# A three-stage transformer kernel: another order and algebra in the feed-forward chain, three PSUM banks for rolled keys, and a router layer placed in the second attention's drain

## The chip, the cores and the metric

The kernel runs on one core of one Trainium2 chip. The metric is device time in microseconds (us) of one execution. A core has five engines that each work through their own queue in order and wait for each other by semaphores: PE (TensorE, matmul), DVE (VectorE), ACT (ScalarE), POOL (GpSimd) and SP, which here only issues DMAs. Matmul results land in PSUM, eight banks of 128 partitions by 512 floats.

## What is computed

The input is 16 sequences of 256 tokens, each a row of 128 floats. Four residual steps follow each other, each on a layer-normalised x.

```python
x = x + attn_a(_layernorm(x))     # 16 heads of 64, causal
x = x + ffn(_layernorm(x))
x = x + attn_b(_layernorm(x))     # in each token its 16 heads of 8 attend to each other
x = x + ffn(_layernorm(x))        # the same weights
```

The feed-forward step routes tokens to 64 slots per sequence, updates the slots with a gated cell, lets the slots attend to each other, and reads them back:

```python
h = gelu(concat([x, slot_mean]) @ w1 + b1)
route_logits = (h @ w2 + b2) / (abs(tau) + 0.1)
topk_vals, topk_idx = top_k(route_logits, 8)
alpha = (one_hot(topk_idx, 64) * softmax(topk_vals)[..., None]).sum(-2)
si = einsum('bts,btd->bsd', alpha, x) / (alpha.sum(1) + 1e-8)[..., None]
i_r, i_z, i_n = split(si @ Wih.T + bih);  h_r, h_z, h_n = split(S @ Whh.T + bhh)
r, z = sigmoid(i_r + h_r), sigmoid(i_z + h_z);  n = tanh(i_n + r * h_n)
S_new = (1 - z) * n + z * S
attn = softmax((S_new @ wq + bq) @ (S_new @ wk + bk).T * DQ**-0.5)
y = S_new + attn @ (S_new @ wv + bv)
slot_values = (layernorm(y) * ln_g + ln_b) @ wvp + bvp
out = (alpha @ slot_values) @ wo + bo
```

## The kernel before

The program is four stages in a row: the first attention (a_tensor and its sisters for the other engines, 16 batches of 4 head groups), the feed-forward stage f_tensor/f_scalar/f_vector/f_gpsimd (called with rep 0), the second attention (b_tensor and sisters, 16 batches, written two to a loop trip), and the feed-forward stage again (rep 1). x stays in SBUF as the tile X, 32 token tiles of 128 by 128.

**What sets the order.** Each engine walks the same hand-written list of steps (a_steps, b_steps, A_PROLOGUE, A_EPILOGUE, B_PROLOGUE, B_EPILOGUE, F_PLAN) and emits its own part of a step, so the lists are the order of every queue. Nothing moves a step at run time: an instruction whose semaphore is late holds back all that is queued behind it on its engine.

**The feed-forward stage** works in two chunks of 8 sequences (16 token tiles). The steps per chunk are: "stats" and "apply" (layer norm of x into f_xs), "hidden" (transposes, first router layer, gelu), "logits", "top" (eight largest, subtract the largest, mark them), "alpha" (exponential and normalisation), "read" (alpha times x, and alpha transposed), "slots", "inputs" (si transposed, times Wih), "gates", "candidate", "new" (the new slots f_sn), "qkv", "scores", "probs", "attend", "ynorm", "values" and "out". F_PLAN lets the chunks alternate, with chunk 1 two steps behind from "gates" on.

Between the first attention and the feed-forward stage stand set_tensor and set_vector: ten small matmuls and some twenty DVE instructions that derive constants from the weights. The statistics of the first 16 tiles ("ffn_stats", "ffn_apply", in the function early_norm) are taken inside the attention stages, the others in the feed-forward stage.

**The second attention** multiplies the query with keys rolled by whole heads. A "roll" step is four PE matmuls into T[j % 2], one of two banks, and one DVE multiplication out of it (b_prod). Two "dots" steps per batch sum the products, each into a bank of its own, M[j]; ACT copies them out, "flip" transposes them. Values are weighed on POOL ("weigh") and summed on DVE ("gather"). The result b_o goes through a scratch tensor in DRAM and comes back in another layout (b_y); "yt" turns it on PE, "project" and "finish" project it, "add" writes X.

**The drain of the second attention** (B_EPILOGUE) ends with two such turnings. The second waits for POOL's last product, its normalisation and the round trip through DRAM.

## Time and profile before

| | us |
|---|---|
| median of 3 runs | 945.12 |
| lowest, highest | 944.6, 946.56 |
| the profiled execution | 945.51 |
| its span, first to last instruction | 943.7 |
| first attention, to the first router transpose | 524.2 |
| feed-forward stage, to the last add | 90.9 |
| second attention, to the router's first transpose | 233.9 |
| feed-forward stage again, with the output | 94.7 |

The profiled execution lies 0.4 us above the median, and 1.8 us of it are outside the span. The profile shows per engine when an instruction ran, how long the engine had been idle before it, and which engine's semaphore ended that idle time. All times below are us from the start of the span. The matmul clock that was granted is given as a share of 2.4 GHz: 1.00 is 2.4 GHz, 0.50 is 1.2 GHz.

### The profile page before, as it was taken

What the parts mean: (1) busy time and instruction counts of PE and PEld (TensorE: products, weight loads), DVE (VectorE), ACT (ScalarE), POOL (GpSimd) and SP (SyncE); (2) the same over time, 40 slices, a digit from 0 to 9 for tenths busy, and PEclk for the clock granted to TensorE, in tenths of its full rate; (3) what the DMA queues carried; (4) which work ended last, traced back from release to release, by engine and by line L of the source; (5) the groups of instructions that cost most, each with busy time, mean ns of one, the idle gap of its engine ahead of it and who ended that gap; (6) DMA issues with size and microseconds to landing.
All of it is one profiled execution on the core that took longest, in us unless ns stands there. A gap on an engine that the chain in (4) does not pass through costs nothing.

```text
span 943.7 us, 25617 instructions
## 1 busy us (share of the span) xinstructions
PE 789.8 (84%) x10324; PEld 606.5 (64%) x10324; DVE 672.3 (71%) x1528; ACT 480.2 (51%) x849; POOL 409.8 (43%) x302
## 2 busy tenths in 40 slices
PE   1899999999999999999986876667888888839655
PEld 0688888888888888888875553534555555525435
DVE  3767667776677766677674776536999999966773
ACT  1678766787767777677752423013444433315220
POOL 1454444544445444454442100116888888751000
PEclk9999999999999999999996778768999999958786
DMA  6000000000000000000000000000221111120002
GB/s 274 1 3 1 0 0 0 0 0 0 0 0 0 0 0 0 0 0 0 1 1 2 0 1 1 1 0 1 23 24 22 22 22 22 20 27 1 1 1 89
DMA packets 71588, 13.25 MB, mean 14 GB/s; under 512 B 66432, under 2 KB 70528, under 8 KB 70912
## 3 DMA queue, kind: packets, MB, share of 16 engines
q1 hardware_dynamic: 71552, 12.76, 6.2%
q8 instruction: 24, 0.39, 0.2%
q14 instruction: 12, 0.10, 0.0%
HBM read 8.56 MB, written 4.19 MB: 14 GB/s over the span
## 4 chain that ended last, share of the span: by engine, by line
PE 63%; DVE 19%; ACT 8%; issue 5%; POOL 3%; DMA 1%; DVEq 0%; ACTq 0%; SPq 0%; POOLq 0%
PE PS L533 6%; PE PS L490 6%; PE PS L349 5%; PE PS L350 4%; PE PS L351 4%; PE PS L426 3%; PE PS L732 3%; DVE b_prod L843 3%; PE PS L722 3%; PE PS L526 2%; PE PS L512 2%; PE PS L724 2%; PE PS L1015 2%; DVE a_nm L607 2%; PE PS L497 2%
## 5 line engine op out<-in xcount | busy, mean ns | idle before, releaser
L640 POOL TENSOR_TENSOR a_pl<-a_p,a_ph 128x1024 f16<-128x1024 f32 (+1 forms) x128 | 210.7, 1646 | 256.3 <-ACT a_ph L562 256.3
L891 POOL TENSOR_TENSOR b_w<-b_v,b_e 128x2048 f32<-128x2048 f32 x32 | 137.8, 4307 | 13.9 <-ACT b_e L811 13.9
L559 ACT ACTIVATE a_p<-PS 128x1024 f32<-128x1024 f32 (+1 forms) x128 | 103.7, 810 | 74.8 <-PE PS L497 74.7
L607 DVE TENSOR_REDUCE a_nm<-PS 128x4 bf16<-128x512 f32 (+1 forms) x128 | 121.5, 949 | 0.0
L843 DVE TENSOR_TENSOR b_prod<-PS,b_qt 128x512 f32<-128x512 f32 x128 | 85.4, 682 | 26.3 <-PE PS L724 22.0
L562 ACT ACTIVATE a_ph<-PS 128x1024 f16<-128x1024 f32 (+1 forms) x128 | 103.1, 805 | 0.0
L552 ACT ACTIVATE a_qk_h<-PS 128x512 f16<-128x512 f32 x128 | 73.4, 604 | 57.1 <-PE PS L351 55.8
L372 POOL TENSOR_TENSOR veps<-mv,eps 128x2 f32<-128x2 f32 (+2 forms) x40 | 8.0, 201 | 190.4 <-DVE mv L1165 136.9
L596 DVE TENSOR_TENSOR a_qk_l<-PS,a_qk_h 128x512 f16<-128x512 f32 x128 | 87.0, 681 | 3.4 <-ACT a_qk_h L552 3.4
L512 PE MATMUL PS<-a_vh,a_ph 128*128 128x65 f16 x768 | 78.5, 196 | 0.3 <-issue 0.3
L514 PE MATMUL PS<-a_vl,a_ph 128*128 128x64 f16 x768 | 78.3, 194 | 0.0
L516 PE MATMUL PS<-a_vh,a_pl 128*128 128x65 f16 x768 | 78.0, 195 | 0.0
L349 PE MATMUL PS<-xhl,a_wqk_h 128*128 128x256 f16 x256 | 70.8, 277 | 8.5 <-ACT xhl L550 7.5
L512 PEld LDWEIGHTS PS<-a_vh,a_ph 128*128 128x128 f16 x768 | 70.5, 98 | 11.1 <-issue 9.5
L858 DVE TENSOR_REDUCE b_s<-b_w 128x128 f32<-128x2048 f32 x32 | 72.8, 2277 | 4.9 <-POOL b_w L891 4.9
L722 PE MATMUL PS<-b_kh,w_rolls 128*128 128x256 f16 x256 | 65.9, 285 | 11.4 <-DVE b_prod L843 8.0
L603 DVE TENSOR_TENSOR a_vl<-PS,a_vh 128x512 f16<-128x512 f32 x64 | 44.3, 692 | 41.8 <-ACT a_vh L555 41.8
L514 PEld LDWEIGHTS PS<-a_vl,a_ph 128*128 128x128 f16 x768 | 71.4, 100 | 0.1
L516 PEld LDWEIGHTS PS<-a_vh,a_pl 128*128 128x128 f16 x768 | 71.4, 98 | 0.0
L351 PE MATMUL PS<-xhl,a_wqk_l 128*128 128x256 f16 x256 | 70.4, 275 | 0.0
L350 PE MATMUL PS<-xhl,a_wqk_h 128*128 128x256 f16 x256 | 70.3, 275 | 0.0
L724 PE MATMUL PS<-b_kl,w_rolls 128*128 128x256 f16 x256 | 65.3, 283 | 0.0
(225 smaller groups left out, 2038.7 us busy)
## 6 DMA issues: line engine op xcount, KB each, us to landing
scratch_dram<-b_o SPq DMA_DIRECT2D x32, 64.0 KB, 3.6
b_y<-scratch_dram SPq DMA_DIRECT2D x16, 128.0 KB, 2.1
out_dram<-X SPq DMA_DIRECT2D x2, 1024.0 KB, 3.9
w_rest<-rest_dram SPq DMA_DIRECT2D x1, 1862.0 KB, 15.2
X<-x_dram SPq DMA_DIRECT2D x1, 1792.0 KB, 11.2
w_first<-first_dram SPq DMA_DIRECT2D x1, 1600.0 KB, 7.1
w_rolls<-rolls_dram SPq DMA_DIRECT2D x1, 544.0 KB, 15.8
X<-x_dram SPq DMA_DIRECT2D x1, 256.0 KB, 3.6
```

Of the source, the lines that this page charges most:

```text
L349: pe.matmul(dst, ah, bh, start=start, stop=False, skip_group_check=True)
L350: pe.matmul(dst, ah, bl, start=False, stop=False, skip_group_check=True)
L351: return pe.matmul(dst, al, bh, start=False, stop=stop, skip_group_check=True)
L512: pe.matmul(O[q][:, h * W:(h + 1) * W], ph[:, nx, par, pair, at], a_vh[:, (g - 1) % GA, k, h, :], start=first, stop=False, skip_group_chec ...
L514: pe.matmul(O[q][:, h * W:h * W + EA], ph[:, nx, par, pair, at], a_vl[:, (g - 1) % GA, k, h, :], start=False, stop=False, skip_group_check ...
L516: ins = pe.matmul(O[q][:, h * W:(h + 1) * W], pl[:, nx, par, pair, at], a_vh[:, (g - 1) % GA, k, h, :], start=False, stop=h == 3 and k == ...
L559: act.activation((a_p0, a_p1)[j][:, me, :, :, :].rearrange("p a h q -> p a (h q)"), TT[:, :, 0:512 - 256 * j], ACT.Exp, scale=EA ** -0.5)
L562: act.activation((a_ph0, a_ph1)[j][:, me, :, :, :].rearrange("p a h q -> p a (h q)"), TT[:, :, 0:512 - 256 * j], ACT.Exp, scale=EA ** -0.5 ...
L607: dve.tensor_reduce(a_nm[:, nx, j, :].rearrange("p (a h) -> p a h", a=2)[:, :, 0:2], MM[:, :, 0:256 * (j + 1)].rearrange("p a (h k) -> p a ...
L640: pool.tensor_tensor(*(n[:, g % 2, :, :, :].rearrange("p a h q -> p (a h q)") for n in (pl, p, ph)), ALU.subtract).then_inc(a_split, 1)
L843: dve.tensor_tensor(b_prod[:, j, :, :], T[j % 2][:, :].rearrange("p (e t) -> p e t", e=2), b_qt[:, 1 - par, :].unsqueeze(1).to_broadcast([ ...
L891: pool.tensor_tensor(b_w8[:, j, :, :, :], rolled_values(par, j, 0, H), rolled_exps(par, j, 0, H), ALU.mult).then_inc(b_weighed, 1)
```

## The change

**Constants.** set_tensor and set_vector are cut in two parts, steps "set" 0 and 1, and moved into the last batch and the epilogue of the first attention. They now use two banks instead of five and no longer build bv_rows; the matrix wcomb gets its column means taken out, which takes one more matmul and two DVE instructions where one stood.

**Norms.** The 32 tiles are normalised in three pieces, PIECES: 16, 12 and 4 tiles. The first stays inside the attention stages (in the second attention its statistics move ahead of two "gather" steps); the statistics of the 12 move in there as well (in the second attention also their normalisation); the last 4 follow the last add. "stats" of a piece on POOL is its own step, "ffn_rstd".

**Router.** "hidden" of chunk 0 uses other banks (PS[2:4] for the transposes, PS[4:6] for the layer) and no longer waits for the last add of X. In the second attention it stands in B_EPILOGUE ahead of the last turning.

**Feed-forward chain.** "top" is cut in two, so that "topa" of chunk 1 precedes "alpha" of chunk 0. The sum over the chosen eight is taken from their own eight exponentials (128 x 16 x 8) and no more from the masked 64. "gates" leaves DVE: the recurrent part gate_h comes into PSUM by a matmul with the identity, and ACT takes the tanh straight from PSUM. bv comes in by a one-row matmul, and ACT copies the values out. The mean of y is folded into wcomb, so the transpose of y is computed by PE directly (the identity times f_sn plus four products) while DVE takes the statistics; the scale rstd is applied with the last addition. "ynorm" is gone. F_PLAN has another order.

**Second attention.** Rolled keys use three banks (PS[2:5]) and both "dots" steps share the fourth, PS[5], in two halves; "dots" 1 therefore waits for the copy of "dots" 0.

The core of the diff:

```diff
+A_EPILOGUE = [("normal", 0, 0), ("turn", 0, 0), ("pv", 0, 0), ("pv", 0, 1), ("normal", 1, 0), ("set", 1, 1), ("turn", 1, 0),
+              ("ffn_stats", 1, 1), ("ffn_rstd", 1, 1), ("project", 1, 0)]
...
-              ("project", 1, 0), ("finish", 1, 0), ("ffn_stats", 0, 0), ("add", 1, 0), ("ffn_apply", 0, 0), ("yt", 1, 0),
+              ("ffn_apply", 0, 0), ("ffn_stats", 0, 1), ("ffn_rstd", 0, 1), ("project", 1, 0), ("finish", 1, 0),
+              ("add", 1, 0), ("ffn_apply", 0, 1), ("hidden", 0, 0), ("yt", 1, 0),
               ("project", 2, 0), ("finish", 2, 0), ("add", 2, 0)]
...
+F_PLAN = [("stats", 2), ("hidden", 0), ("apply", 1), ("apply", 2), ("logits", 0), ("hidden", 1), ("logits", 1),
+          ("topa", 0), ("topb", 0), ("topa", 1), ("expo", 0), ("expo", 1), ("alpha", 0), ("read", 0), ("topb", 1), ("slots", 0),
+          ("inputs", 0), ("wih", 0), ("alpha", 1), ("gates", 0), ("candidate", 0), ("read", 1), ("new", 0), ("slots", 1),
+          ("qkv", 0), ("inputs", 1), ("scores", 0), ("wih", 1), ("gates", 1), ("probs", 0), ("candidate", 1), ("attend", 0),
+          ("new", 1), ("qkv", 1), ("values", 0), ("scores", 1), ("out", 0), ("probs", 1), ("attend", 1), ("add", 0),
+          ("values", 1), ("out", 1), ("add", 1)]
+PIECES = [(0, CT), (CT, CT - 4), (NT - 4, 4)]
...
-                    wait(pe, b_multiplied, m - 1)
+                    wait(pe, b_multiplied, m - 1 if j < 2 else m - 2)
...
-                    wait(pe, b_raised, 2 * b + j + 1)
+                    wait(pe, b_raised, 2 * (b + 1) + j)
...
+                elif kind == "wih":
+                    pe.wait_ge(f["alt_ev"], k)
+                    for n in range(2):
+                        pe.matmul(B[2 + n][:, :].rearrange("p (b s) -> p b s", s=NS), ident[:, :],
+                                  gate_h[:, n:n + 1, :].to_broadcast([128, CB, NS]), start=True, stop=False)
...
+                    pe.matmul(B[2][:, :], ident[:, :], v["sn"][:, :], start=True, stop=False, skip_group_check=True)
...
+                        ins = pe.matmul(B[2][:, sl], v["v"][:, p, :], v["pt"][:, sl], start=False, stop=p == PAIRS - 1,
+                                        skip_group_check=True)
```

On DVE, at the end of the first attention, the constants (brz to crow) stood behind the last addition to X. This is the queue before, from the chunk's normalisation on:

```order
L377 TENSOR_SCALAR f_xs0<-X,mv,rstd 128x128 x16
L616 RECIPROCAL a_rs<-PS 128x8
L617 TENSOR_TENSOR a_o<-PS,a_rs 128x512
L616 RECIPROCAL a_rs<-PS 128x8
L617 TENSOR_TENSOR a_o<-PS,a_rs 128x512
L623 TENSOR_TENSOR X<-PS,X 128x256
L1218 TENSOR_TENSOR brz<-w_rest 128x2
```

And the same place in the changed kernel, from the last constant of part 0 to the last of part 1 (eight instructions between inv_tau and c1 are left out):

```order
L1270 TENSOR_SCALAR wsum<-PS,w_rest 128x128
L381 TENSOR_SCALAR f_xs0<-X,mv,rstd 128x128 x16
L632 RECIPROCAL a_rs<-PS 128x8
L633 TENSOR_TENSOR a_o<-PS,a_rs 128x512
L632 RECIPROCAL a_rs<-PS 128x8
L633 TENSOR_TENSOR a_o<-PS,a_rs 128x512
L1272 SCALAR_TENSOR_TENSOR inv_tau<-w_rest 65x1
```

```order
L1282 TENSOR_TENSOR c1<-PS,w_rest 64x1
L1283 SCALAR_TENSOR_TENSOR wcomb<-PS,wsum 128x128
L1284 COPY crow<-PS 128x128
L368 BN_STATS stats<-X 128x6 x12
L370 MEMSET gate 128x1
L372 BN_AGGR mv<-stats 128x2 x12
L639 TENSOR_TENSOR X<-PS,X 128x256
```

Part 0 moved ahead of f_xs0, part 1 and the statistics of 12 tiles ahead of the last addition to X.

On PE, at the end of the second attention, the turning of b_y (L747, then L752, L757 and L763 for its projection) stood ahead of the router (L923 transposes f_xs0, L1015 is the layer). Before:

```order
L747 MATMUL PS<-w_first,b_y 128x128 x2
L752 MATMUL PS<-b_bo_h,ones_h 128x256
L752 MATMUL PS<-b_bo_l,ones_h 128x256
L757 MATMUL PS<-X,w_first 128x128 x2
L763 MATMUL PS<-w_rest,b_yt 128x128 x2
L923 MATMUL PS<-w_first,f_xs0 128x128 x8
L1015 MATMUL PS<-f_xt,w_rest 64x512
```

In the changed kernel, where the turning is L765 and the router L957 and L935:

```order
L957 MATMUL PS<-w_first,f_xs0 128x128 x4
L935 MATMUL PS<-f_xt,w_rest 64x512 x2
L765 MATMUL PS<-w_first,b_y 128x128 x2
L770 MATMUL PS<-b_bo_h,ones_h 128x256
L770 MATMUL PS<-b_bo_l,ones_h 128x256
L775 MATMUL PS<-X,w_first 128x128 x2
L781 MATMUL PS<-w_rest,b_yt 128x128 x2
L976 MATMUL PS<-w2s,f_h 128x64 x16
```

The whole router layer of chunk 0 stands ahead of the last turning, and the logits (L976) follow the projection at once.

On DVE, at the end of the feed-forward stage, chunk 1's softmax (f_rs1, f_p1) stood behind the statistics and the normalised y of chunk 0. Before:

```order
L1171 TENSOR_SCALAR f_y0<-PS,mv,rstd 128x128 x4
L1151 TENSOR_REDUCE f_rs1<-f_s1 128x4
L1152 RECIPROCAL f_rs1<-f_rs1 128x4
L1155 TENSOR_TENSOR f_p1<-f_s1,f_rs1 64x4x64 x2
L1176 TENSOR_TENSOR f_so0<-PS,crow 128x512
L1162 BN_STATS stats<-PS 128x6 x4
L1165 BN_AGGR mv<-stats 128x2 x4
L1184 TENSOR_TENSOR X<-PS,X 128x2x256 x4
L1171 TENSOR_SCALAR f_y1<-PS,mv,rstd 128x128 x4
L1176 TENSOR_TENSOR f_so1<-PS,crow 128x512
```

In the changed kernel:

```order
L1187 TENSOR_SCALAR f_k1<-PS,w_rest 32x512
L1217 SCALAR_TENSOR_TENSOR f_so0<-PS,rstd,crow 128x128 x4
L1191 TENSOR_REDUCE f_m1<-PS 128x4
L1192 TENSOR_TENSOR f_s1<-PS,f_m1 128x256
L1196 TENSOR_REDUCE f_rs1<-f_s1 128x4
L1197 RECIPROCAL f_rs1<-f_rs1 128x4
L1200 TENSOR_TENSOR f_p1<-f_s1,f_rs1 64x4x64 x2
L1207 BN_STATS stats<-PS 128x6 x4
L1210 BN_AGGR mv<-stats 128x2 x4
L1226 TENSOR_TENSOR X<-PS,X 128x2x256 x4
L1217 SCALAR_TENSOR_TENSOR f_so1<-PS,rstd,crow 128x128 x4
```

f_y0 and f_y1 are gone, and chunk 0's values f_so0 stand ahead of chunk 1's whole softmax.

## Rows read from the trace of the kernel before

**Rows 1.** The page: granted clock in 40 slices, and the last chain by engine.

```profile
PEclk9999999999999999999996778768999999958786
...
PE 63%; DVE 19%; ACT 8%; issue 5%; POOL 3%; DMA 1%; DVEq 0%; ACTq 0%; SPq 0%; POOLq 0%
```

**Rows 2.** Busy time per stage: from:to, length, busy (instructions) per engine, clock, DMA.

```profile
0.00:524.20 524.20, 478.17 (x7988) 404.23 (x7988) 356.50 (x730) 345.70 (x545) 229.14 (x176) 0.98 0.03 13
524.20:615.10 90.90, 65.79 (x392) 44.99 (x392) 59.60 (x231) 25.88 (x40) 5.55 (x6) 0.76 0.00 1
615.10:849.00 233.90, 181.31 (x1553) 112.88 (x1553) 196.61 (x338) 82.69 (x224) 169.56 (x114) 0.91 0.16 19
849.00:943.70 94.70, 64.55 (x392) 44.35 (x392) 59.56 (x231) 25.89 (x40) 5.55 (x6) 0.77 0.06 23
```

**Rows 3.** Timeline of PE, 500 to 537: start, length, what, idle before it.

```profile
506.84 1.09 PE L526 MATMUL PS<-w_first,a_o 128*128 128x128 f32 x4 [6.61 <-DVE a_o L617]
...
512.88 5.39 PE L533 MATMUL PS<-w_rest,a_ot 128*128 128x128 f32 x32 [0.78 <-ACT a_ot L566]
...
524.21 1.97 PE L923 MATMUL PS<-w_first,f_xs 128*128 128x128 f32 x8 [1.14 <-DVE crow L1239]
...
532.88 3.79 PE L933 MATMUL PS<-w2s,f_h 65*128 65x64 f32 x32
```

**Rows 4.** Timeline of DVE, 499 to 536.

```profile
499.04 6.82 DVE L377 TENSOR_SCALAR f_xs<-X,mv,rstd 128x128 f32<-128x128 f32 x16 [2.31 <-POOL rstd L373]
...
523.88 0.27 DVE L1239 COPY crow<-PS 128x128 f32<-128x128 f32 x1
...
531.77 4.20 DVE L377 TENSOR_SCALAR f_xs<-X,mv,rstd 128x128 f32<-128x128 f32 x16 [3.32 <-POOL rstd L373]
```

**Rows 5.** Busy time of PE alone in two stretches: busy, clock, DMA.

```profile
524.20:530.00 5.80, 5.79 (x16) 0.51 0.00 0
530.00:536.70 6.70, 6.70 (x44) 1.00 0.00 0
```

**Rows 6.** Timeline of PE, the drain and the second stage's router.

```profile
837.41 0.66 PE L747 MATMUL PS<-w_first,b_y 128*128 128x128 f32 x2 [8.98 <-DMA b_y<-scratch_dram]
...
844.52 0.66 PE L747 MATMUL PS<-w_first,b_y 128*128 128x128 f32 x2 [3.90 <-DMA b_y<-scratch_dram]
...
857.39 3.88 PE L933 MATMUL PS<-w2s,f_h 65*128 65x64 f32 x32
...
868.65 3.79 PE L933 MATMUL PS<-w2s,f_h 65*128 65x64 f32 x32
```

**Rows 7.** Timeline of DVE at the same place.

```profile
836.99 3.18 DVE L364 BATCH_NORM_STATS2 stats<-X 128x6 f32<-128x128 f32 x16
...
844.70 4.19 DVE L377 TENSOR_SCALAR f_xs<-X,mv,rstd 128x128 f32<-128x128 f32 x16 [3.33 <-POOL rstd L373]
...
861.30 2.20 DVE L1087 MAX8 f_v<-PS 128x8 f32<-128x64 f32 x16 [0.59 <-PE PS L933]
```

**Rows 8.** Timeline of PE in the second feed-forward stage.

```profile
875.99 3.71 PE L941 MATMUL PS<-f_xs,f_al 128*64 128x129 f32 x32 [3.56 <-DVE f_al L1103]
...
890.22 1.99 PE L941 MATMUL PS<-f_xs,f_al 128*64 128x129 f32 x32 [0.67 <-DVE f_al L1103]
...
895.93 2.84 PE L957 MATMUL PS<-f_sit,w_rest 128*128 128x512 f32 x6 [1.73 <-ACT f_sit L1045]
...
924.54 2.06 PE L1007 MATMUL PS<-f_so,f_alt 64*128 64x128 f32 x32
```

**Rows 9.** Timeline of DVE in the same stage: chunk 1's new slots, and the end.

```profile
906.28 0.69 DVE L1135 SCALAR_TENSOR_TENSOR f_sn<-f_zg,f_n 128x512 f32<-128x512 f32 x1
...
938.14 1.29 DVE L1184 TENSOR_TENSOR X<-PS,X 128x512 f32<-128x512 f32 x2 [0.42 <-PE PS L1007]
```

**Rows 10.** Timeline of DVE in one batch of the second attention's loop.

```profile
742.40 3.56 DVE L843 TENSOR_TENSOR b_prod<-PS,b_qt 128x512 f32<-128x512 f32 x5
...
747.64 1.45 DVE L843 TENSOR_TENSOR b_prod<-PS,b_qt 128x512 f32<-128x512 f32 x2 [0.15 <-PE PS L724]
```

More of the change, by code:

```diff
@@ L97, in a_steps, with b_steps @@
         put(g == 1 and not first, ("project", 0))
-        put(last and g == 2, ("ffn_stats", 0))
-        put(last and g == 3, ("ffn_apply", 0))
+        put(last and g == 2, ("ffn_stats", 0), ("ffn_rstd", 0))
+        put(last and g == 3, ("set", 0), ("ffn_apply", 0))
     return steps
-def b_steps(par, former=True, before=True, third=True, ahead=True, ahead2=True):
+def b_steps(par, former=True, before=True, third=True, ahead=True, ahead2=True, tail=False):
     one, two = ahead, ahead2
@@ L128, in b_steps @@
     put(True, "sumexp")
+    put(tail, ("ffn_stats", 0), ("ffn_rstd", 0))
     put(one, ("roll", 5), ("dots", 0))
@@ L167 @@
           (b_steps(0) + b_steps(1), 2, NB // 2 - 3),
-          (b_steps(0, ahead2=False) + b_steps(1, ahead=False, ahead2=False), NB // 2 - 1, None),
+          (b_steps(0, ahead2=False) + b_steps(1, ahead=False, ahead2=False, tail=True), NB // 2 - 1, None),
           (B_EPILOGUE, NB // 2, None)]
-F_PLAN = [("stats", 1), ("hidden", 0), ("apply", 1), ("logits", 0), ("hidden", 1),
-          ("logits", 1), ("top", 0), ("alpha", 0), ("read", 0), ("top", 1), ("slots", 0), ("inputs", 0), ("alpha", 1),
-          ("read", 1), ("gates", 0), ("slots", 1), ("inputs", 1)]
-LATER = ["gates", "candidate", "new", "qkv", "scores", "probs", "attend", "ynorm", "values", "out"]
-F_PLAN.append(("candidate", 0))
-for n in range(2, len(LATER) + 2):
-    F_PLAN += [(LATER[m], c) for m, c in ((n, 0), (n - 2, 1)) if m < len(LATER)]
+F_PLAN = [("stats", 2), ("hidden", 0), ("apply", 1), ("apply", 2), ("logits", 0), ("hidden", 1), ("logits", 1),
[4 more added lines that the diff above has]
+          ("values", 1), ("out", 1), ("add", 1)]
+EARLY = [(), (("hidden", 0), ("apply", 1))]
+PIECES = [(0, CT), (CT, CT - 4), (NT - 4, 4)]
 class Fill:
@@ L743, in do @@
                     ins.then_inc(b_flipped, 1)
+                elif kind == "hidden":
+                    hidden_tensor(pe, 1, 0, CHUNKS + 1)
                 elif kind == "yt":
@@ L915, in do @@
                 if kind == "hidden":
[L916 to L927 removed]
+                    hidden_tensor(pe, rep, c, k)
                 elif kind == "logits":
@@ L1191, in do @@
                 if kind == "stats":
-                    pool.wait_ge(f["stats"], k)
-                    norm_rstd(pool, chain.link, CT).then_inc(f["rstd"], 1)
+                    rstd_piece(pool, chain.link, rep, c)
                 elif kind == "attend":
@@ L1322, in _ @@
             a_tensor(pe)
-            set_tensor(pe)
+            pe.wait_ge(consts_set, 1)
             f_tensor(pe, 0)
```

304 lines of the change are left out of this document (165 added, 139 removed).

## The prediction

> **What bounds the kernel now.** I read the page first. The last chain is 63% PE and 19% DVE, and the granted clock is full through the first attention and ragged behind it [rows 1]. Then busy time by stage [rows 2]. In the first attention PE is busy 478 of 524 us: PE sets the pace, and the change leaves its loop alone. In the second attention DVE is busy 196.6 of 233.9 us; within the loop it hardly waits at all: in one batch its only idle time is 0.15 us ahead of a product of rolled keys [rows 10]. In each of the two feed-forward stages no engine is busy for more than 66 of 91 to 95 us: they are bound by latency, by one engine handing over to the next. So a change of order, or an instruction less on the chain, is worth its full time there, and next to nothing inside the loops. That leaves four places: the two stretches ahead of the router, and the two chains behind it.
>
> I cost each against its own stretch of the profiled execution (945.5 us, of which 943.7 are the span; the median of the runs is 0.4 us lower).
>
> **End of the first attention.** Now: DVE normalises the first chunk from 499.04 to 505.86, PE turns at 506.84, projects at 512.88, and the router starts at 524.21, waiting for crow [rows 3, 4]. The projection ends at 518.27, so the constants cost 5.9 us on the path. The change puts part 0 of them ahead of the normalisation, where DVE waits 2.3 us for POOL anyway. But part 0 needs PE, and PE is at the last scores until 500.2. Its six matmuls take about 1.1 us there, DVE's six instructions about 1.4 us: the normalisation starts at 502.8 instead of 499.0. It then takes less time. The first four of its 16 instructions needed 3.7 us beside POOL's last differences, which end at 502.7; 16 without them take 4.20 us [rows 4]. It ends at 507.0, 1.2 us later than now. Part 1's four matmuls (1.5 us at half clock) stand ahead of the second turning, which waits for DVE for 1.1 us in any case: 0.4 us more. DVE's share of part 1 and the statistics of 12 tiles (3.4 us) run beside the 5.4 us of projection. So projection ends at 519.8, and the router follows it at once, its input long ready: 524.2 - 519.8 = **4.4 us**.
>
> The Trainium skill has a rule on this overlap (GPSIMD Engine Reference, Specifications): GpSimd shares its SBUF interfaces with VectorE, and collides with instructions in a two-port mode or with two SBUF inputs. The trace agrees with its 6.82 against 4.20 us [rows 4]. Without it the normalisation would keep its 6.8 us and this term would be 1.8 us.
>
> **The router's clock.** The router now begins on a PE that has paused: 0.51 until 530, 1.00 after [rows 5]. From its start to the end of logits 0 it takes 12.4 us (524.21 to 536.67 [rows 3]). Behind an unbroken projection I expect it at full clock, 10.3 us: transposes at 0.6, layers at 0.9, the table load of 1.3 and logits of 3.7. Gain **2.1 us**, between 0 and 3.
>
> **Drain of the second attention.** Now logits 0 end at 861.2 [rows 6]: the last turning (844.52), its projection, then the router. PE idles 9 us and 3.9 us ahead of the two turnings for data from DRAM [rows 6], and DVE idles 3.3 us for POOL [rows 7]. The change takes the statistics before two gathers, where DVE stands waiting for POOL's products (2.3 us and 2.6 us of such waits). The second gather still ends at 837.0, since POOL's product ends at 834.8. What POOL pays: rstd of 16 (3.2 us) is now queued ahead of its normalisation of the last batch, which starts at 838.0, not 837.15. So the last turning's data arrive near 845.4. That is covered, because PE is then in the router: the normalisation runs 838.0 to 842.2, the router 842.2 to about 850 (half clock at first), the turning and its projection (3 us) until 852.3, logits 0 until 855.6. Gain 861.2 - 855.6 = **5.6 us**. The last 4 tiles' norm (1.3, 1.4, 1.1 us) ends at 857.5, just when group 3 of the second router layer wants it. If the cover fails (the router late), the last turning is late one for one.
>
> **The feed-forward chain**, from the end of logits 0 (L) to the last addition, now takes 939.4 - 861.2 = 78.2 us [rows 6, 9]; the first stage is within 0.3 us of it. In it chunk 1's new slots are ready at L + 45.8 (906.97), and 32.5 us follow [rows 9]. Worked out anew, with DVE and PE queues in the new order:
> - Logits 1 end at L + 11.3, as now (868.65 + 3.79 [rows 6]). Topa 1 is 3.7 (2.2 of it for the maxima [rows 7]), alpha 0 is 3.0 (a sum over 8 instead of 64 saves 1), read 0 at half clock 3.7 [rows 8], slots 1.25, transposes 0.6, ACT 1.5: L + 25.
> - Two matmuls with the identity (1.8) and three with Wih (2.8 at full clock [rows 8]): L + 29. Here the change adds PE work; it takes 1.3 us of DVE additions away. Read 1 with its transposes 3.0, bv, q, k and v 3.0, transposes of si and ACT 1.2, again 4.6 for the gates: L + 41. Candidate, tanh, chunk 0's statistics between, and new: L + 47. Nothing is won for chunk 1 up to here; chunk 0 is 6 us ahead of where it was.
> - Behind that, PE has q, k, v of chunk 1, values 0 and scores 1 (3.9), DVE so 0 (1.3, ahead of chunk 1's scores), then scores 0.9, exp 0.4, softmax 1.5, transposes and ACT 1.3, attend 3.5 with the direct transpose of y, ACT 0.6, values 1.1, so 1 behind half an addition 1.6, out 2.1 at full clock [rows 8], last addition 1.2: 19.4.
>
> Together 66.4 us against 78.2: **11.8 us** for each stage. The 13 us come out of the tail, where now the two chunks' last steps, normalised y, its transposes at half clock and the statistics between, stand in one row. The bounds are the clock: if PE stayed at 1.2 GHz in this tail, its 11 us would be 16 to 20, and the gain 5; if slots and inputs overlapped as well as they can, 14.
>
> **Three banks.** DVE loses 0.15 us in a batch [rows 10], over 14 batches 2.1 us; PE, no longer held by the product before last, has the sixth rolled keys 0.6 us sooner. In the prologue PE is at half clock and slower than DVE, so nothing. **2 us**, between 0 and 3. The shared bank costs nothing while dots 1 starts 2.0 us after the copy of dots 0 has ended.
>
> **Sum:** 4.4 + 2.1 + 5.6 + 2 x 11.8 + 2 = 37.7 us. From 945.5 that is 907.8, and 907.4 by the median: I take **907 us**.
>
> **Rivals.**
> - *The chain becomes one of PE at half clock.* For it: eight more matmuls of 512 columns in each stage (four for the gates, two for the transpose of y, two for bv), and the clock falls whenever PE waits [rows 1, 8]. Against: the pauses that make it fall are what the change shortens. It would take 5 to 7 us from each stage's gain and the 2.1 of the router: 907 + 14 = 921 us.
> - *Only placing helps.* The queue for chunk 0 waits for topa 1, so alpha 0 comes 3 us later behind L than now, and if the interleaved chunks hinder each other all the way as they do up to L + 47, only half of the tail's 13 us stays in each stage: 907 + 13 = 920 us.
> - *More than I count:* the router at full clock in both stages, attend's two halves overlapped, ACT's copies hidden: 4 us more in each stage, 899 us.
> - *Slower than before:* the shared "dots" bank. It makes dots 1 wait for ACT's copy of dots 0. If that copy came over 2.0 us later than now, all 14 batches would lengthen one for one; to eat 38 us it must come 2.0 + 2.7 = 4.7 us late in every batch. At 5 us late: 907 + 14 x 3 = 949 us. ACT has 2.5 us idle ahead of this copy, which speaks against it.
> - *No change:* the gains would have to be given back wholly, for instance by statistics and norm pieces that hold DVE at the drain. I see no place for 38 us.
>
> **How the numbers follow.** Forecast (900 to 914) 0.70; PE at half clock 0.10; only placing 0.09; more than counted 0.08; no change 0.01; slower 0.02. The likeliest gives 907. The range 899 to 917 leaves out the outer halves of the two rivals that are slower than the forecast, and the last two. A measurement of this kernel can tell about 0.2% from no change: faster 0.97, same 0.01, slower 0.02.
>
> **What would show it.** The first router transpose near 519.8, and a clock near 1.00 in the six us after it. The first stage's last addition near 596 (now 615.1). A loop of the second attention with no idle time before the seventh product. In the drain the router's transposes 6.7 us earlier than now, in the pause before the last turning, and logits 0 over by about 5.6 us sooner counted from the last gather. From new slots of chunk 1 to the last addition 19 to 20 us in each stage, with a clock of 0.9 or more. I am wrong if the clock in the feed-forward stages stays at 0.76, or if alpha 0 or wih 1 comes more than 3 us later than listed.

## The result, and the profile after

The changed kernel takes 898.2 us (median of 3 runs, 898.0 to 898.6) against 945.1: ratio 0.950, 95% interval [0.948, 0.952], 46.9 us less. I had forecast 907 (899 to 917), so the measured time lies just below my range. The direction and most steps were right; one term was sized at a fifth of what it is worth.

The page after, clock line and chain, against [rows 1]:

```profile
PEclk9999999999999999999999787987999999977799
...
PE 66%; DVE 15%; ACT 7%; issue 6%; POOL 4%; DMA 1%; DVEq 0%; ACTq 0%; SPq 0%; POOLq 0%
```

The same four stages after, to be read beside [rows 2] (from:to, length, busy (instructions) per engine, clock, DMA). The borders are the first router transpose, the end of the last addition, and in the last stage the end of logits 0. In [rows 2] the last border is the router's first transpose, 12 us ahead of the end of logits 0, so the last two rows do not match in length; the table below uses the same borders for both:

```profile
0.00:522.82 522.82, 480.84 (x7989) 406.38 (x7990) 356.30 (x753) 345.50 (x545) 231.27 (x178) 0.98 0.03 13
522.82:598.33 75.51, 60.60 (x418) 41.16 (x416) 49.59 (x202) 27.02 (x42) 4.46 (x6) 0.93 0.00 1
598.33:826.80 228.47, 188.69 (x1610) 119.87 (x1611) 199.75 (x385) 88.34 (x233) 173.00 (x118) 0.92 0.17 19
826.80:896.40 69.60, 50.61 (x361) 34.84 (x358) 44.51 (x179) 21.07 (x33) 3.21 (x4) 0.90 0.08 31
```

The feed-forward stages shrink and their clock rises from 0.76 and 0.77 to 0.93 and 0.90. That was expected. The surprise is in the second attention.

**Where the 47.3 us of the two spans went.** L is the end of logits 0, as in the prediction.

| stretch | before | after | gain | forecast |
|---|---|---|---|---|
| start and first attention's loop | | 1.6 later | -1.6 | 0 |
| end of first attention, router, logits 0 | L at 536.7 | L at 533.0, 1.6 of it the shift | 5.3 | 6.5 |
| first chain, L to last addition | 78.4 | 65.3 | 13.1 | 11.8 |
| second attention, to its last gather | 222.0 | 209.2 | 12.7 | 2 |
| drain, last gather to L | 24.2 | 19.2 | 5.0 | 5.6 |
| second chain | 78.2 | 65.3 | 12.8 | 11.8 |

The first row is a shift that is there early and then stays. The same addition in both traces, DVE's timeline, first of before, then of after:

```profile
99.44 0.42 DVE L623 TENSOR_TENSOR X<-PS,X 128x256 f32 x1 [2.25 <-PE PS L533]
484.46 0.42 DVE L623 TENSOR_TENSOR X<-PS,X 128x256 f32<-128x256 f32 x1 [2.91 <-PE PS L533]
```

```profile
101.07 0.42 DVE L639 TENSOR_TENSOR X<-PS,X 128x256 f32 x1 [2.24 <-PE PS L545]
486.08 0.42 DVE L639 TENSOR_TENSOR X<-PS,X 128x256 f32<-128x256 f32 x1 [2.90 <-PE PS L545]
```

It is 1.63 us at 100 us and 1.62 at 485, so no loop makes it. In the trace of experiment 7, whose edit touches nothing ahead of the second attention's drain, the same addition stands at 99.49, so the shift differs from one profiled execution to the next.

**The term that failed.** One batch of the second attention's loop after the change, against [rows 10], DVE's timeline:

```profile
729.23 3.07 DVE L863 TENSOR_TENSOR b_prod<-PS,b_qt 128x512 f32<-128x512 f32 x5
...
733.20 2.00 DVE L863 TENSOR_TENSOR b_prod<-PS,b_qt 128x512 f32<-128x512 f32 x3
```

The idle 0.15 us ahead of the seventh product is gone, as forecast. But the five products for which the timeline named *no* idle time take 3.07 instead of 3.56 us. One product is 0.68 to 0.69 us long in both kernels. So they stood (3.56 - 0.69)/4 = 0.72 us apart in the mean and now stand 0.60 apart.

The timeline names a pause only from 0.15 us on and merges rows across shorter ones; other views count them. Here is the busy time of the five products in their own window, first before, then after:

```profile
742.40:745.96 3.56, 3.31 (x5) 1.00 0.00 0
```

```profile
729.23:732.30 3.07, 3.07 (x5) 1.00 0.00 0
```

And the eight products of the same batch before as a group, with all the idle time ahead of them (0.5 us) and what of it is put down to PE (0.2):

```profile
L843 DVE TENSOR_TENSOR b_prod<-PS,b_qt 128x512 f32<-128x512 f32 x8 | 5.3, 681 | 0.5 <-PE PS L724 0.2
```

So 0.25 of the lost 0.49 us are two short pauses of DVE, 0.11 us ahead of the third product and 0.14 ahead of the fifth. The other half shows as no pause at all, since a late product starts where the record of the one before is still running. Product by product the distances were 0.60, 0.79, 0.66 and 0.83 us; now all four are 0.60. A batch lasts 11.5 us (729.23 to 740.75, first product to first product) instead of 12.25.

### The profile page after: what moved, and what is told of

Its sections match the earlier page's. It is cut to its first block, busy times and chain, and to the rows that moved or that the text cites. A ratio compares the mean times of both kernels' runs of the same rounds, so it can differ in the third digit from the quotient of the medians.

```text
span 896.4 us, 25703 instructions
## 1 busy us (share of the span) xinstructions
PE 780.7 (87%) x10372; PEld 602.2 (67%) x10372; DVE 650.1 (73%) x1518; ACT 481.9 (54%) x853; POOL 411.9 (46%) x306
## 4 chain that ended last, share of the span: by engine, by line
PE 66%; DVE 15%; ACT 7%; issue 6%; POOL 4%; DMA 1%; DVEq 0%; ACTq 0%; SPq 0%; POOLq 0%
PE PS L545 7%; PE PS L502 6%; PE PS L353 6%; PE PS L354 4%; PE PS L355 4%; PE PS L434 4%; POOL b_w L911 3%; DVE b_prod L863 3%; PE PS L538 3%; PE PS L524 3%; PE PS L748 2%; PE PS L738 2%; PE PS L509 2%; PE PS L528 2%; DVE a_nm L623 2%
## 5 line engine op out<-in xcount | busy, mean ns | idle before, releaser
L911 POOL TENSOR_TENSOR b_w<-b_v,b_e 128x2048 f32<-128x2048 f32 x32 | 137.7, 4306 | 13.1 <-ACT b_e L829 13.1
L863 DVE TENSOR_TENSOR b_prod<-PS,b_qt 128x512 f32<-128x512 f32 x128 | 80.3, 676 | 18.5 <-PE PS L740 17.8
L376 POOL TENSOR_TENSOR veps<-mv,eps 128x2 f32<-128x2 f32 (+3 forms) x42 | 9.0, 215 | 166.8 <-DVE mv L1210 119.4
L526 PE MATMUL PS<-a_vl,a_ph 128*128 128x64 f16 x768 | 78.2, 194 | 0.0
## 6 DMA issues: line engine op xcount, KB each, us to landing
X<-x_dram SPq DMA_DIRECT2D x1, 1792.0 KB, 11.5
```

What stands on the lines that cost most here:

```text
L526: pe.matmul(O[q][:, h * W:h * W + EA], ph[:, nx, par, pair, at], a_vl[:, (g - 1) % GA, k, h, :], start=False, stop=False, skip_group_check ...
L863: dve.tensor_tensor(b_prod[:, j, :, :], ROLLED[j % 3][:, :].rearrange("p (e t) -> p e t", e=2), b_qt[:, 1 - par, :].unsqueeze(1).to_broadc ...
L911: pool.tensor_tensor(b_w8[:, j, :, :, :], rolled_values(par, j, 0, H), rolled_exps(par, j, 0, H), ALU.mult).then_inc(b_weighed, 1)
```

## Experiment 1: which part of the change is it?

Theory A: with two banks, a product waits for a roll that itself waits for the product before last, and this round trip sets the distance of the products. About half of it hides below the length of one instruction, because a ready successor starts before the record of its predecessor ends. Theory B: the banks only give the visible idle time, and the rest comes from the moved statistics.

The kernel before with the three banks (and the bank that the dots then share), and nothing else:

```diff
-                    wait(pe, b_multiplied, m - 1)
+                    wait(pe, b_multiplied, m - 1 if j < 2 else m - 2)
-                        pe.matmul(T[j % 2][:, e * SEQ:(e + 1) * SEQ], ...
+                        pe.matmul(ROLLED[j % 3][:, e * SEQ:(e + 1) * SEQ], ...
-                            ins = pe.matmul(M[j][32 * n:32 * n + 32, 0:SEQ], ...
+                            ins = pe.matmul(DOTS[32 * n:32 * n + 32, j * SEQ:(j + 1) * SEQ], ...
```

> The kernel before with one part of the change alone: rolled keys in three banks (roll j waits for product j-2), both dots in the fourth. Theory A (with two banks each product waited for a roll that could start only after the product before the last one had ended, and this round trip, about 0.70 us, set the distance of the products although the profile shows DVE as busy throughout; with three it falls to DVE's own 0.60): a group of five products takes 3.07 us instead of 3.56, a batch 11.5 us instead of 12.25, and the time is 10 to 13 us below the kernel before, 932 to 935. Theory B (the banks only take away the 0.15 us of idle time that the trace shows, as predicted, and the rest of the gain in this stage is from the statistics and waits that the change moved): 2 to 3 us, 942 to 943, products still 0.70 apart.

Measured: 934.0 us, ratio 0.987 [0.984, 0.990]. Its DVE timeline in one batch:

```profile
735.58 3.07 DVE L844 TENSOR_TENSOR b_prod<-PS,b_qt 128x512 f32<-128x512 f32 x5
```

The reverse, the changed kernel with the two banks back (the same diff read from below):

> The changed kernel with two banks for rolled keys and a bank for each dots, as before; all else stays. Theory A: the batch is 12.2 us again, the second attention 10 to 13 us longer, the time 908 to 911. Theory B: 2 to 3 us, 900 to 901.

Measured: 910.8 us, ratio 0.963 [0.959, 0.966]; against 0.950 of the changed kernel that is 11.8 us lost.

```profile
736.98 3.56 DVE L862 TENSOR_TENSOR b_prod<-PS,b_qt 128x512 f32<-128x512 f32 x5
...
742.23 1.45 DVE L862 TENSOR_TENSOR b_prod<-PS,b_qt 128x512 f32<-128x512 f32 x2 [0.16 <-PE PS L739]
```

Both ways the banks are worth 11 to 12 us. Theory B is out.

## Experiment 2: the bank, or the moment of release?

Three banks, but every roll waits as late as before:

```diff
-                    wait(pe, b_multiplied, m - 1 if j < 2 else m - 2)
+                    wait(pe, b_multiplied, m - 1)
```

> The changed kernel with its three banks, but each roll again waits for the product just before the last one that it follows (m - 1 for every roll), so the third bank is never used early. If the order of release is the cause (theory A): as with two banks, 908 to 911, products 0.70 apart in the groups of five. If it is the bank itself (two engines in the same two banks), the gain stays: about 898 to 900.

Measured: 910.5 us, ratio 0.963 [0.960, 0.966], and in the trace the old rhythm:

```profile
735.68 3.56 DVE L863 TENSOR_TENSOR b_prod<-PS,b_qt 128x512 f32<-128x512 f32 x5
```

So it is not that two engines met in one bank. The third bank is worth nothing by itself; it is worth the permission to start a roll one product earlier.

## Experiment 3: changing the round trip itself

Shorter: the kernel before without the two low-half matmuls of each roll.

```diff
-                        pe.matmul(T[j % 2][:, e * SEQ:(e + 1) * SEQ], w["roll"][:, 2 * j + e, :], b_kh[:, nx, :], ...
-                        ins = pe.matmul(T[j % 2][:, e * SEQ:(e + 1) * SEQ], w["roll"][:, 2 * j + e, :], b_kl[:, nx, :], ...
+                        ins = pe.matmul(T[j % 2][:, e * SEQ:(e + 1) * SEQ], w["roll"][:, 2 * j + e, :], b_kh[:, nx, :], ...
```

> The kernel before without the two matmuls of each roll that take the keys' low half (the rolled keys are then of lower precision; this part of the computation is left out). Two banks stay, but the round trip from product to product is 2 matmuls of about 0.11 us shorter. Theory A: products then stand DVE's own 0.60 apart with two banks, the batch loses at least 0.7 us from this and the time is 10 to 13 us down, plus what PE's 16 x 0.11 = 1.8 us less work in a batch gives where PE sets the pace. Theory B: products stay 0.70 apart, and only the groups in which DVE is seen idle (0.15 us) shorten, 2 to 4 us in all.

Longer: the first matmul of each roll twice, in the kernel before and in the changed one.

```diff
                     for e in range(2):
+                        if e == 0:
+                            pe.matmul(T[j % 2][:, 0:SEQ], w["roll"][:, 2 * j, :], b_kh[:, nx, :], start=True, ...
```

> The kernel before with one matmul more in each roll (the first is issued twice, the second overwrites it), so the round trip from product to product is 0.11 us longer; two banks stay. Theory A (the round trip sets the distance): products 0.80 to 0.82 us apart instead of 0.70, idle time now shown between them, about 0.7 to 0.9 us more in each of 16 batches: 956 to 960. Rival (VectorE's own speed sets the distance and PE has room): 945 to 947.

> The changed kernel with the same additional matmul in each roll. With three banks a roll has two products' time, about 1.2 us, for a round trip of 0.8: theory A expects the distance to stay 0.60 and the time within 2 us of the changed kernel, 897 to 901. If PE's own work were what sets the pace of the batch (8 matmuls of 0.11 more, 0.9 us a batch): 910 to 913.

Measured, as groups on DVE's timeline. Without the low half (935.5 us, ratio 0.988 [0.985, 0.991]):

```profile
735.88 3.14 DVE L841 TENSOR_TENSOR b_prod<-PS,b_qt 128x512 f32<-128x512 f32 x5
```

Before with the longer roll (952.7 us, ratio 1.008 [1.006, 1.010]):

```profile
743.88 1.28 DVE L845 TENSOR_TENSOR b_prod<-PS,b_qt 128x512 f32<-128x512 f32 x2
745.37 2.29 DVE L845 TENSOR_TENSOR b_prod<-PS,b_qt 128x512 f32<-128x512 f32 x3 [0.22 <-PE PS L726]
...
749.55 1.45 DVE L845 TENSOR_TENSOR b_prod<-PS,b_qt 128x512 f32<-128x512 f32 x2 [0.37 <-PE PS L726]
```

Changed kernel with the longer roll (904.6 us, ratio 0.956 [0.953, 0.959]):

```profile
750.02 3.14 DVE L865 TENSOR_TENSOR b_prod<-PS,b_qt 128x512 f32<-128x512 f32 x5
...
754.84 1.45 DVE L865 TENSOR_TENSOR b_prod<-PS,b_qt 128x512 f32<-128x512 f32 x2 [0.16 <-PE PS L742]
```

| kernel | banks | matmuls in a roll | mean distance in the five |
|---|---|---|---|
| before, low half left out | 2 | 2 | (3.14 - 0.69)/4 = 0.61 |
| before | 2 | 4 | (3.56 - 0.69)/4 = 0.72 |
| before, longer roll | 2 | 5 | (3.78 - 0.69)/4 = 0.77 |
| changed | 3 | 4 | (3.07 - 0.69)/4 = 0.60 |
| changed, longer roll | 3 | 5 | (3.14 - 0.69)/4 = 0.61 |

The mechanism holds and my arithmetic on record for the longer roll does not. I wrote that 0.11 us more in the roll is 0.11 us more per product, 956 to 960. With two banks, the round trip reaches from the end of product j - 2 to the start of product j and so covers *two* distances. With R for the time from the end of product j - 2 to the start of product j, d = (0.69 + R)/2. From 0.72, R is 0.745 us. One matmul more gives (0.69 + 0.855)/2 = 0.77, measured 0.77. Two fewer give (0.69 + 0.525)/2 = 0.61, measured 0.61; this point is weak alone, since DVE's own 0.60 is as near. The single products show the step more sharply. From the first product's start to the third's it was 1.39 us and is 1.49 with one matmul more, from the third's to the fifth's 1.49 and 1.59: one matmul's 0.11 us in each round trip. With three banks the bound is (0.69 + 0.745)/3 = 0.48, below the 0.60 at which DVE follows itself, so within the five DVE sets the pace.

The changed kernel with the longer roll missed too: 897 to 901 expected, 904.6 measured. Here the five products stay near 0.6 as expected, but the 0.16 us of idle ahead of the seventh are back and a batch lasts 11.82 us (744.39 to 756.21, gather to gather). That is 0.3 us in 14 batches, some 4 us. PE's queue ahead of that roll holds the first dots (741.00 to 742.07) and a turning (to 742.44), which three banks do not shorten. The rest of the miss is within the spread of that kernel's runs (901.2 to 908.3); the traced one is the slowest of them.

**What is left of the 12.7 us.** From the first stage's last addition to the last gather it is 222.0 us before, 211.2 with only the banks added, 219.9 in the changed kernel with two banks, 209.2 in the changed kernel. So the banks carry 10.7 us and the other parts 2.0. These 2.0 lie in the prologue. PE's windows over the 17 us behind the last addition, first before, then after:

```profile
615.10:632.10 17.00, 10.79 (x56) 0.50 0.00 0
```

```profile
598.33:615.33 17.00, 9.79 (x64) 0.70 0.00 1
```

In the same time PE gets through 64 instead of 56 instructions, at a mean clock of 0.70 instead of 0.50. In the kernel before with three banks it is 0.50 again, in the changed kernel with two 0.70. The old order of experiment 4, with three banks and all the rest of the change, has 0.51 and 211.2 us. So these 2.0 us come with the new order of the feed-forward stage and not with the moved statistics: it leaves PE's clock higher, and the next stage starts with it.

## Experiment 4: the feed-forward chain, order against algebra

The changed kernel's steps, put in the order of the kernel before, but for one place. Chunk 1 goes two steps behind chunk 0, and as "ynorm" is gone from the list, chunk 0's "out" now comes ahead of chunk 1's "attend", where it stood behind it:

```diff
-          ("inputs", 0), ("wih", 0), ("alpha", 1), ("gates", 0), ("candidate", 0), ("read", 1), ("new", 0), ("slots", 1),
...
+          ("inputs", 0), ("wih", 0), ("alpha", 1), ("read", 1), ("gates", 0), ("slots", 1), ("inputs", 1), ("wih", 1), ("gates", 1),
+          ("candidate", 0)]
+LATER = ["gates", "candidate", "new", "qkv", "scores", "probs", "attend", "values", "out", "add"]
+for n in range(2, len(LATER) + 2):
+    F_PLAN += [(LATER[m], c) for m, c in ((n, 0), (n - 2, 1)) if m < len(LATER) and (m or not c)]
```

> The changed kernel's steps of the feed-forward stages (the constants' matmuls, the direct transpose of y, the norm folded into the values' addition), but put in the order of the kernel before: alpha 0 and read 0 ahead of topa 1, inputs, gates and candidate one behind the other, and behind them chunk 1 two steps behind chunk 0 all the way, so that its last steps stand in one row. If most of the 13 us of a stage come from the order of the tail (as the prediction has it): the tail from chunk 1's new slots is 5 to 8 us longer than the 19.2 us of the changed kernel, of which alpha 0 in front gives 4 back at the head, and the time is 900 to 908. If the steps that are gone carry the gain: the tail is at most 3 us longer, and the time is 890 to 896.

Measured: 928.5 us, ratio 0.982 [0.981, 0.984], 30 us above the changed kernel and 20 worse than the worst I had given. L to the last addition takes 80.0 us, against 78.4 before and 65.3 after: **in this order, the new algebra gains nothing**. From chunk 1's new slots on, its DVE timeline, and PE's two output groups:

```profile
577.36 0.69 DVE L1184 SCALAR_TENSOR_TENSOR f_sn<-f_zg,f_n 128x512 f32<-128x512 f32 x1
...
602.81 0.89 DVE L1208 BATCH_NORM_STATS2 stats<-PS 128x6 f32<-128x128 f32 x4 [7.54 <-PE PS L1037]
...
608.87 2.48 DVE L1227 TENSOR_TENSOR X<-PS,X 128x512 f32<-128x512 f32 x4 [1.26 <-PE PS L1058]
```

```profile
596.37 3.79 PE L1058 MATMUL PS<-f_so,f_alt 64*128 64x128 f32 x32
600.08 0.79 PE L1036 MATMUL PS<-f_v,f_pt 128*128 128x128 f32 x2
...
607.66 2.06 PE L1058 MATMUL PS<-f_so,f_alt 64*128 64x128 f32 x32 [1.29 <-DVE f_so L1218]
```

The tail is 33.3 us, as long as the 32.5 of before [rows 9]. Chunk 0's whole output (3.79 us, at half clock) stands ahead of chunk 1's attention (L1036), and DVE idles 7.5 us until that is done. In the kernel before, chunk 1's attention had come first, ahead of the output at 924.54 [rows 8]:

```profile
922.66 0.39 PE L986 MATMUL PS<-f_v,f_pt 128*128 128x128 f32 x2
```

So up to some 4 of the 80.0 us, an estimate from the length of that output, belong to this one place and not to the old order. The algebra may be worth that much without the new order, and no run shows it. In the changed kernel the tail is 19.2 us:

```profile
872.26 0.69 DVE L1183 SCALAR_TENSOR_TENSOR f_sn<-f_zg,f_n 128x512 f32<-128x512 f32 x1
...
889.64 2.48 DVE L1226 TENSOR_TENSOR X<-PS,X 128x512 f32<-128x512 f32 x4 [1.26 <-PE PS L1057]
```

How the order saves 14.7 us for the same work is in PE's windows from L to the last addition: the old order first, then the changed kernel, then the kernel before:

```profile
531.31:611.35 80.04, 60.66 (x360) 0.81 0.00 1
```

```profile
826.80:892.12 65.32, 50.61 (x361) 0.92 0.04 17
```

```profile
861.27:939.43 78.16, 52.27 (x336) 0.78 0.03 14
```

360 and 361 instructions are the same work. In the old order PE is busy with it 10.1 us longer, at a clock of 0.81 instead of 0.92, and idle 4.7 us longer. So two thirds of what this order gives arrive as clock. That PE's pauses are what lets it fall is argued from where they stand, and not shown by a run of its own. Before to after, PE's idle time falls by 11.2 us while 25 more instructions cost it 1.7 us *less*. In the old order part of the additional matmuls are paid at half clock, those of chunk 0's gates (0.85 us apart instead of 0.43) and of chunk 1's bv; the others, the transposed y among them, run at full clock there too. Whether one could have the clock without the order was not tried.

## Experiment 5: what the new order leaves on the table

PE idles 6.70 us ahead of read 0 in the changed kernel, because alpha 0 queues behind topa 1. This is the point where my own schedule had the order lose 3 us and take them back later.

```diff
-          ("topa", 0), ("topb", 0), ("topa", 1), ("expo", 0), ("expo", 1), ("alpha", 0), ("read", 0), ("topb", 1), ("slots", 0),
-          ("inputs", 0), ("wih", 0), ("alpha", 1),
+          ("topa", 0), ("topb", 0), ("expo", 0), ("alpha", 0), ("topa", 1), ("expo", 1), ("read", 0), ("slots", 0),
+          ("topb", 1), ("inputs", 0), ("wih", 0), ("alpha", 1),
```

> The changed kernel with another order in both feed-forward stages: exp 0 and alpha 0 ahead of the maxima of chunk 1 (topa 1), slots 0 ahead of topb 1. In the changed kernel PE stands idle for 6.7 us ahead of read 0, because alpha 0 is queued on VectorE behind topa 1, which waits for logits 1. Theory A (this queue is on the path): read 0 starts about 4.4 us sooner behind logits 0, PE's pause shrinks to about 2 us, and each stage is 3 to 5 us shorter: 888 to 892. Rival: chunk 1 is the late one, and alpha 1 and its read come as late as now or later; then nothing or a loss of 1 to 2 us: 898 to 901.

Measured: 890.5 us, ratio 0.942 [0.940, 0.945]. Read 0 in the second stage, PE's timeline, first the changed kernel, then this one:

```profile
843.46 3.71 PE L984 MATMUL PS<-f_xs,f_al 128*64 128x129 f32 x32 [6.70 <-DVE f_al L1155]
```

```profile
835.59 3.41 PE L984 MATMUL PS<-f_xs,f_al 128*64 128x129 f32 x32 [2.55 <-DVE f_al L1155]
```

L to the last addition falls from 65.3 to 61.1 us in both stages, 8.4 in the trace and 7.4 by the ratios. The forecast gain of the order was right in sum, but this part of it was a loss that could be avoided.

## Experiment 6: the end of the first attention

The prediction had DVE start the normalisation at 502.8 and the projection end at 519.8. In the trace of after (1.6 us to be taken off for the shift), DVE and then PE:

```profile
503.73 0.48 DVE L1266 TENSOR_SCALAR gate_h<-PS,brz 128x64 f32<-128x64 f32 x2 [5.31 <-PE PS L1252]
...
504.97 4.17 DVE L381 TENSOR_SCALAR f_xs<-X,mv,rstd 128x128 f32<-128x128 f32 x16
```

```profile
510.13 1.09 PE L538 MATMUL PS<-w_first,a_o 128*128 128x128 f32 x4 [6.51 <-DVE a_o L633]
...
513.12 0.37 PE L1255 MATMUL PS<-slot_mean,w_rest 128*64 128x1 f32 x2
...
515.45 1.06 PE L538 MATMUL PS<-w_first,a_o 128*128 128x128 f32 x4
517.29 5.69 PE L545 MATMUL PS<-w_rest,a_ot 128*128 128x128 f32 x32 [0.78 <-ACT a_ot L578]
522.82 1.04 PE L957 MATMUL PS<-w_first,f_xs 128*128 128x128 f32 x8
...
529.21 3.79 PE L976 MATMUL PS<-w2s,f_h 65*128 65x64 f32 x32
```

DVE stands 5.31 us ahead of six matmuls that PE reaches only after the last scores, with the whole normalisation behind it, and PE then stands 6.51 us. The projection ends at 522.98 - 1.62 = 521.4, a gain of 2.9 instead of 4.4. I had 1.2 us of delay for the turning; it was 510.13 - 1.62 - 506.84 = 1.7. And part 1's matmuls, with PE at half clock, took 2.3 us (513.12 to 515.45) where I had 1.5. Together these are 1.3 of the 1.5 us. The test puts both out of the way at once, so it does not tell them apart: statistics behind the row maxima of the last heads, PE's part 0 in a pause, the normalisation between the two turnings.

```diff
         put(True, ("maxrow", 0))
+        put(last and g == 3, ("ffn_stats", 0), ("ffn_rstd", 0))
...
-        put(last and g == 2, ("ffn_stats", 0), ("ffn_rstd", 0))
-        put(last and g == 3, ("set", 0), ("ffn_apply", 0))
-A_EPILOGUE = [("normal", 0, 0), ("turn", 0, 0), ("pv", 0, 0), ("pv", 0, 1), ("normal", 1, 0), ("set", 1, 1), ("turn", 1, 0),
+A_EPILOGUE = [("normal", 0, 0), ("turn", 0, 0), ("setm", 0, 0), ("ffn_apply", 0, 0), ("pv", 0, 0), ("pv", 0, 1),
+              ("normal", 1, 0), ("setv", 0, 0), ("turn", 1, 0), ("set", 1, 1),
```

Here setm is PE's half of part 0, and setv is DVE's.

> The changed kernel with another order at the end of the first attention: statistics of chunk 0 behind the row maxima of the last heads (they hold these up by 3.5 us now, and PE idles 3.3 us for them), PE's part 0 of the constants behind the turning of the second-last heads and VectorE's behind the normalisation of the last heads, the first chunk's normalisation (4.2 us) between the two turnings, part 1 behind the last turning. VectorE now waits 5.3 us for PE's part 0 with the whole normalisation queued behind. If this queue is what ate 1.6 of the predicted 4.4 us, the projection ends 5 to 8 us sooner than in the changed kernel and the time is 891 to 894. If the router's input or VectorE becomes late instead (the row f_xs behind 515), 0 to 3 us: 895 to 898.

Measured: 894.2 us, ratio 0.946 [0.943, 0.949]. PE's timeline:

```profile
511.04 5.87 PE L545 MATMUL PS<-w_rest,a_ot 128*128 128x128 f32 x32
516.75 1.04 PE L957 MATMUL PS<-w_first,f_xs 128*128 128x128 f32 x8
```

The router starts 6.1 us sooner in the trace; by the ratios the gain is 4.2 us, with intervals of about 3 us on it. The normalisation now takes 6.21 us, beside POOL's differences, against 4.17 alone:

```profile
500.25 6.21 DVE L381 TENSOR_SCALAR f_xs<-X,mv,rstd 128x128 f32<-128x128 f32 x16
```

The prediction had the same from [rows 4]: 6.82 and 4.20 there. The single records show how it comes about. In the kernel before, the first of the 16 takes 2.14 us instead of 0.34 and ends with POOL's difference at 501.1, and one more takes 1.17; the other 14 keep their pace. So one VectorE instruction is held until POOL's has ended, and the rest lose nothing.

## Experiment 7: the router ahead of the last turning

In the changed kernel, DVE and PE in the drain:

```profile
808.43 4.48 DVE L381 TENSOR_SCALAR f_xs<-X,mv,rstd 128x128 f32<-128x128 f32 x16 [0.88 <-POOL rstd L377]
```

```profile
812.98 1.97 PE L957 MATMUL PS<-w_first,f_xs 128*128 128x128 f32 x8 [1.38 <-DVE f_xs L381]
...
821.44 0.44 PE L765 MATMUL PS<-w_first,b_y 128*128 128x128 f32 x2
...
823.12 3.68 PE L976 MATMUL PS<-w2s,f_h 65*128 65x64 f32 x32
```

The test removes hidden 0 from the drain, so it stands behind the last projection:

```diff
-              ("add", 1, 0), ("ffn_apply", 0, 1), ("hidden", 0, 0), ("yt", 1, 0),
+              ("add", 1, 0), ("ffn_apply", 0, 1), ("yt", 1, 0),
-EARLY = [(), (("hidden", 0), ("apply", 1))]
+EARLY = [(), (("apply", 1),)]
```

> The changed kernel with the last stage's first router layer behind the second attention's last turning and projection, as before, all else as changed. If the order is worth what I ascribed to it (the router runs in PE's pause ahead of the last turning): logits 0 end 3 to 5 us later, 901 to 903. If the gain in the drain is from the statistics and normalisation alone, which stay early here: 898 to 899.

Its PE timeline:

```profile
814.36 0.66 PE L765 MATMUL PS<-w_first,b_y 128*128 128x128 f32 x2 [4.35 <-DMA b_y<-scratch_dram]
...
824.70 3.79 PE L976 MATMUL PS<-w2s,f_h 65*128 65x64 f32 x32
```

Last gather to L is 828.5 - 806.2 = 22.3 us here, 19.2 in the changed kernel, 24.2 before. So of 5.0 us in the drain, 3.1 are the router's place and 1.9 the earlier statistics and normalisation. The measured time, 905.1 us with ratio 0.958 [0.954, 0.962], is some 4 us more than this explains and above my 901 to 903. Its four executions fall in two pairs, 899.9 and 901.6 at a mean granted clock of 0.955, and 908.6 twice at 0.942 and 0.941; only the first was traced. I take the 3.1 us from the trace, and leave open where the second pair lost its clock.

## Both improvements together

Experiments 5 and 6 in one kernel:

> Both edits, of the feed-forward order and of the end of the first attention. They touch different stretches, so the gains should add up within 1 us: 881 to 886 if both work.

Measured: 888.2 us, ratio 0.938 [0.935, 0.941]: 11.5 us below the changed kernel, where the two alone gave 7.4 and 4.2. The sum holds, but 888.2 misses my 881 to 886, which was for the sum of the traces. In this trace the clock fell at 522 us, in the middle of logits 0, which take 4.61 instead of 3.79 us:

```profile
522.56 4.61 PE L976 MATMUL PS<-w2s,f_h 65*128 65x64 f32 x32
```

The first stage's chain takes 64.6 us for it, the second's 61.1. The last try moves part 1 of the constants behind the last projection:

```diff
-              ("normal", 1, 0), ("setv", 0, 0), ("turn", 1, 0), ("set", 1, 1),
-              ("ffn_stats", 1, 1), ("ffn_rstd", 1, 1), ("project", 1, 0)]
+              ("normal", 1, 0), ("setv", 0, 0), ("turn", 1, 0),
+              ("ffn_stats", 1, 1), ("ffn_rstd", 1, 1), ("project", 1, 0), ("set", 1, 1)]
```

> The kernel with both orders improved (e7), and part 1 of the constants behind the last projection instead of ahead of it, with the waits for the constants at the first uses (ACT's first gelu, PE's logits). The projection no longer waits for 2.3 us of half-clock matmuls; they take about 1.2 us at full clock ahead of the router: 1 to 2 us below e7's trace, a span of 884 to 885 where the granted clock is the same. If gelu 0 then waits for the constants: as e7 or 1 us slower.

Measured: 886.7 us, ratio 0.937 [0.935, 0.939], and a span of 887.3 against 885.9. The router starts at 515.76 instead of 516.17, 0.4 us and not 1 to 2; ACT's first copy then waits for the constants (517.41, released by crow). The span misses my 884 to 885, and the difference to the kernel without it is not measurable. Either is 11 to 13 us faster than the changed kernel.

## Why the prediction was right or wrong, point by point

- **Three banks, 2 us (0 to 3): wrong, 10.7.** The step that failed is "DVE loses 0.15 us in a batch". I took the idle time named in [rows 10] for all that DVE lost to PE, so the wait of each roll for the product before last had no price in my sum; experiments 1 to 3 show that it set the distance of the products, 0.72 us with two banks and 0.60 with three. The same rows show more: five products in 3.56 us. And [rows 9] show two additions of the same 128x512 shape in 1.29 us, so 0.60 us apart at 0.69 us length. Five products at that distance are 3.09 us; the 0.47 us too much, and 0.23 in the other three, were there to be read, 0.7 us in each of some 15 batches. With 10.7 in place of 2 the sum would have been 46.4 us, against 46.9 measured. That they agree so well is luck: the other misses, from -1.6 to +2.3 us, nearly cancel.
- **End of the first attention, 4.4: mis-sized, 2.9.** The two causes are in experiment 6.
- **Router's clock, 2.1: right.** First transpose to logits 0 is 10.2 us (I had 10.3), against 12.4; the gain is 2.2 to 2.4 us.
- **Feed-forward chain, 11.8 each: right mechanism, 13.1 and 12.8.** Tail 19.2 us (19.4 on record), new slots of chunk 1 at L + 46.1 (L + 47 on record). So the chain is 65.3 us where I had 66.4, most of the difference ahead of the new slots. I had not said that most of it comes as clock; experiment 4 shows that, and shows that my rival "the chain becomes one of PE at half clock" comes true in part with this algebra in the old order, at a mean clock of 0.81.
- **Drain, 5.6: right mechanism, 5.0.** The last turning comes straight behind the router, as said. The router began at 812.98, 5.4 us behind the last gather; I had 5.2. It took 8.5 us where I had 7.8. My sum there was wrong in itself: 850 and 3 us of turning and projection are 853, not 852.3, and with logits of 3.8 us it ends at 856.8, which is a gain of 4.4. The measured 5.0 lie between.
- **Prologue "nothing": wrong by 2.0.** I had PE at half clock there; it is at 0.70 on average, as the new order of the stage before leaves it.
- **Start:** a shift of -1.6 us, not caused by anything in the loops, that no row of before could tell.
- Of the rivals, "more than I count" named the right time (899) for the wrong reasons. The shared bank for the dots cost nothing, as forecast: in the batch above, ACT's copy of dots 0 ends at 733.35, and dots 1 start at 735.33, 2.0 us later, released by the last product.

## What to carry to other kernels

No idle time *named* in a trace does not mean that an engine sets the pace: pauses can be too short for the view, or lie under the records. Compare the distance of its instructions with that of ready instructions of the same shape, and where a ring of n buffers feeds it, work out (length + round trip)/n before calling a buffer worthless. In a latency-bound chain, change the order first and count PE's pauses: here the clock gave back more (10.1 us of busy time) than the pauses themselves (4.7), and some of the matmuls that were added without closing the pauses were paid at the lower clock.
